# A decoder on one core: order of norm, turns and features at the beginning, and the first queries by band at the entry of the first cross-attention

## The reference, cut to what matters

```
x = x + L0_attn(layernorm(x))                 # linear attention, 16 heads of 8, cumulative sums over time
x = x + L0_xattn(layernorm(x), ctx, mask)     # softmax cross-attention, 16 heads, 256 keys per batch
x = x + L0_ffn(layernorm(x))                  # 8 experts, top 2, two loops
x = x + L1_attn(layernorm(x))                 # state-space scan
x = x + L1_xattn(layernorm(x), ctx, fside, mask)
x = x + L1_ffn(layernorm(x))                  # quantised feed-forward

# L0_attn: q, k, v, g = heads(x Wq), heads(x Wk), heads(x Wv), sigmoid(x Wg + bg)
# qf = softplus(q) * (g + 1e-6); kf = softplus(k)
# num = qf . cumsum(kf v^T); den = qf . cumsum(kf) + 1e-6; out = (num / den) Wo
# L0_xattn: softmax(q k^T / sqrt(8), key mask) v Wo
```

## Time and profile before

| | us |
|---|---|
| three runs | 608.24, 608.61, 612.67 |
| median of the runs | 608.61 |
| the profiled execution | 611.73 |
| its span, first to last instruction | 610.0 |

### The profile page before, as it was taken

The page is one execution under the profiler, slowest core; times in us unless marked ns, Lnnn a source line. Parts: engine busy times, 40 slices in busy tenths (PEclk is TensorE's granted clock), DMA queues, the critical chain, the costliest instruction groups (busy, mean ns, idle before and its releaser), DMA issues.

```text
span 610.0 us, 9155 instructions
## 1 busy us (share of the span) xinstructions
PE 526.7 (86%) x3260; PEld 298.6 (49%) x3268; DVE 452.4 (74%) x1175; ACT 263.2 (43%) x455; POOL 134.5 (22%) x101
## 2 busy tenths in 40 slices
PE   3997799999999999999999944655668999999886
PEld 1344666665666566566665500222224655555433
DVE  6599667676575366676456789999996778889786
ACT  5531256556433144243243346555521454444553
POOL 8443000000000000040000018899990100000100
PEclk9999799999998899999999985987788999999899
DMA  5000070000010000100000000000001000000001
GB/s 131 24 16 1 18 225 3 1 2 2 6 38 1 1 0 2 34 6 1 1 0 2 1 0 0 0 0 1 1 0 44 2 1 2 2 2 1 2 5 30
DMA packets 10768, 9.26 MB, mean 15 GB/s; under 512 B 2050, under 2 KB 9540, under 8 KB 10724
## 3 DMA queue, kind: packets, MB, share of 16 engines
q1 hardware_dynamic: 10724, 8.69, 5.0%
HBM read 6.98 MB, written 0.52 MB: 12 GB/s over the span
## 4 chain that ended last, share of the span: by engine, by line
PE 66%; DVE 23%; issue 5%; ACT 4%; POOL 2%; POOLq 0%; DVEq 0%; ACTq 0%
PE PS L1154 18%; PE PS L716 10%; PE PS L1180 9%; PE PS L779 5%; DVE PS L1713 5%; DVE VA L1726 5%; PE PS L764 3%; PE PS L755 3%; DVE PS L1719 2%; PE PS L692 2%; PE PS L736 2%; PE PS L455 1%; PE PS L287 1%; PE PS L433 1%; PE PS L789 1%
## 5 line engine op out<-in xcount | busy, mean ns | idle before, releaser
L1154 PE MATMUL PS<-XNT,KSA 128*128 128x512 f32 x256 | 121.5, 609 | 0.0
L941 ACT ACTIVATE E<-PS 128x512 f32<-128x512 f32 x128 | 71.2, 596 | 67.2 <-PE PS L764 41.7
L1168 DVE TENSOR_TENSOR E<-E,PS 128x512 f32<-128x512 f32 x64 | 43.9, 687 | 58.5 <-ACT E L1162 57.5
L1162 ACT ACTIVATE E<-PS 128x512 f32<-128x512 f32 x64 | 38.1, 597 | 108.4 <-PE PS L1154 108.2
L764 PE MATMUL PS<-QM,KP 32*128 32x256 f32 x512 | 81.3, 399 | 0.8 <-ACT E L941 0.8
L716 PE MATMUL PS<-KP,QP 32*128 32x256 f32 x512 | 78.6, 412 | 0.4 <-ACT QP L908 0.4
L1180 PEld LDWEIGHTS PS<-KSA,E 128*128 128x128 f32 x512 | 62.4, 192 | 16.8 <-issue 15.5
L1154 PEld LDWEIGHTS PS<-XNT,KSA 128*128 128x128 f32 x256 | 46.2, 195 | 42.8 <-issue 42.8
L1180 PE MATMUL PS<-KSA,E 128*128 128x128 f32 x512 | 62.4, 275 | 0.4 <-DVE XN L1389 0.4
L716 PEld LDWEIGHTS PS<-KP,QP 32*128 32x128 f32 x512 | 51.5, 191 | 20.8 <-issue 10.3
L292 PE MATMUL PS<-KSA,select 128*128 128x512 bf16 x62 | 24.9, 489 | 41.3 <-ACT KSA L1614 31.2
(11 more groups left out here) (280 smaller groups left out, 859.6 us busy)
## 6 DMA issues: line engine op xcount, KB each, us to landing
KSA<-in_w SPq DMA_DIRECT2D x2, 1024.0 KB, 6.9
X<-in_x SPq DMA_DIRECT2D x2, 256.0 KB, 3.3
SCR<-in_ctxT SPq DMA_DIRECT2D x1, 512.0 KB, 5.6
KP<-OT SPq DMA_DIRECT2D x16, 32.0 KB
SCR<-in_fside SPq DMA_DIRECT2D x1, 512.0 KB, 4.6
KP<-QM SPq DMA_DIRECT2D x16, 32.0 KB
out_x<-X SPq DMA_DIRECT2D x8, 64.0 KB, 1.5
wx<-in_w_x SPq DMA_DIRECT2D x1, 384.0 KB, 6.6
```

What stands on the lines that cost most here:

```text
L941: act.activation(slot(m, j), weight_bank(m, j), ACT.Exp).then_inc(sig("exps"), 1)
L1154: ins = pe.matmul(bank(2 * (g % 3) + o), w[:, e, c * P:(c + 1) * P], XNT[:, tokens_of(p)], start=True, stop=True)
L1162: act.activation(E6[:, 4 + g % 2, :], bank(2 * (g % 3)), ACT.Silu).then_inc(sig("silu"), 1)
L1168: dve.tensor_tensor(E6[:, g % 4, :], E6[:, 4 + g % 2, :], bank(2 * (g % 3) + 1), ALU.mult)\
```

## The change

At the beginning, VectorE does half 0's statistics and variance, half 1's statistics alone, half 0's tiles, and only then half 1's aggregation, variance and tiles. ScalarE computes half 0's root ahead of any key clearing, `by_head` ahead of half 1's root, and clears bands 0 and 1 behind the first copy, band 2 behind the second, and band 3 behind `pair(0)`. TensorE issues 16 products of the identity with itself (128x128, float32) ahead of the first turn; the second half's turn moves behind `features(0)`, and `context_keys` behind `features(1)`.

At the entry for L = 0, TensorE issues ten 128x512 bf16 products of the identity ahead of the turns and three behind them (`turn_ident`, into bank 7), behind two waits (`x_self`, `const_late`). `queries(0)` is replaced by `first_queries` of bands 0 and 1, as for L = 1, and of bands 2 and 3 after the scores. `turn_mixed(pe, 1)` moves behind the scores, which wait for `weighed_sum` instead (VectorE has read banks 3 to 5). ScalarE takes the queries in four copies, with `take_mixed(act, 1)` between the second and the third.

```diff
         def entry_variance(dve, ch, e, half):
             s = slice(4 * half, 4 * half + 4)
-            if e == 0:
-                dve.wait_ge(sig(("x_first", "x_second")[half]), 16)
             for j in range(s.start, s.stop):
                 ins = dve.bn_stats(st[:, j, :], X[:, j, :])
             ch.link(ins)
+            entry_spread(dve, ch, half)
+        def input_stats(dve, half):
+            dve.wait_ge(sig(("x_first", "x_second")[half]), 16)
+            for j in range(4 * half, 4 * half + 4):
+                ins = dve.bn_stats(st[:, j, :], X[:, j, :])
+            ins.then_inc(sig("input_stats"), 1)
+        def entry_spread(dve, ch, half):
+            s = slice(4 * half, 4 * half + 4)
             for j in range(s.start, s.stop):
                 ins = dve.bn_aggr(mv[:, j, :], st[:, j, :])
...
+        def turn_ident(pe, n):
+            for _ in range(n):
+                pe.matmul(bank(7), identb[:, :], identb[:, :].unsqueeze(1).to_broadcast([P, 4, P]),
+                          start=True, stop=True)
...
             features(0)
+            entry_turn(pe, 0, 1)
+            features(1)
             context_keys(pe)
-            features(1)
...
                 pair(b)
                 if b == 0:
+                    keys_clear(act, (3,))
                     keys_take(act, 0)
...
             def first_queries(gs):
-                pe.wait_ge(sig("xnt"), 2 * 5 + 1)
+                pe.wait_ge(sig("xnt"), 2 * (1, 5)[L] + 1)
                 for g in gs:
                     if g >= 2:
-                        pe.wait_ge(sig("query_taken"), g - 1)
-                    pe.matmul(first_query(g), WP[:, 1, g, :], XNT[:, 0:S], start=True, stop=True)\
+                        pe.wait_ge(sig("query_taken"), L * (NG - 1) + g - 1)
+                    pe.matmul(first_query(g), WP[:, L, g, :], XNT[:, 0:S], start=True, stop=True)\
                         .then_inc(sig("query_part"), 1)
...
-                if i == 0 and L == 1 and b == 0 and g < NG - 1:
-                    pe.wait_ge(sig("query_taken"), g + 1)
+                if i == 0 and b == 0 and g < NG - 1:
+                    pe.wait_ge(sig("query_taken"), L * (NG - 1) + g + 1)
...
             if L == 1:
                 turn_over(pe, 2, 16)
+            else:
+                pe.wait_ge(sig("x_self"), 1)
+                pe.wait_ge(sig("const_late"), 1)
+                turn_ident(pe, 10)
             entry_turn(pe, L + 1, 0)
-            if L == 0:
-                queries(0)
+            if L == 1:
+                turn_over(pe, 2, 2)
             else:
-                turn_over(pe, 2, 2)
-                first_queries((0, 1))
+                turn_ident(pe, 3)
+            first_queries((0, 1))
...
             else:
-                turn_mixed(pe, 1)
+                pe.wait_ge(sig("weighed_sum"), NT)
             for i in range(HG):
                 scores(0, i)
             if L == 0:
+                turn_mixed(pe, 1)
+            first_queries((2, 3))
+            if L == 0:
                 project_mixed(pe, 1)
                 context_values(pe)
-            else:
-                first_queries((2, 3))
             queries(1)
...
             entry_take(act, L + 1, 0)
+            for g in range(NG):
+                act.wait_ge(sig("query_part"), L * NG + g + 1)
+                ins = act.activation(QP[:, g, 0:S], first_query(g), ACT.Identity, bias=rowbias[:, L, 0, g:g + 1],
+                                     scale=DH ** -0.5)
+                if g < NG - 1:
+                    ins.then_inc(sig("query_taken"), 1)
+                if g == 1 and L == 0:
+                    take_mixed(act, 1)
+                if g == 1 and L == 1:
+                    entry_root(act, ch, 2, 1)
+            ins.then_inc(sig("queries"), 1)
             if L == 0:
-                take_queries(0)
-                take_mixed(act, 1)
                 context_scalar(act)
                 entry_root(act, ch, 1, 1)
...
             pe.wait_ge(sig("ident"), 1)
+            for _ in range(16):
+                pe.matmul(bank(0)[:, 0:P], ident[:, :], ident[:, :], start=True, stop=True)
             entry_turn(pe, 0, 0)
-            entry_turn(pe, 0, 1)
             self_tensor(pe)
...
             exp_and_ln(act)
+            entry_root(act, ch, 0, 0)
+            by_head(act)
+            entry_root(act, ch, 0, 1)
+            entry_take(act, 0, 0)
             keys_clear(act, (0, 1))
-            entry_root(act, ch, 0, 0)
-            entry_root(act, ch, 0, 1)
-            by_head(act)
-            entry_take(act, 0, 0)
             entry_take(act, 0, 1)
-            keys_clear(act, (2, 3))
+            keys_clear(act, (2,))
...
-            entry_variance(dve, ch, 0, 0)
-            entry_variance(dve, ch, 0, 1)
+            input_stats(dve, 0)
+            dve.wait_ge(sig("input_stats"), 1)
+            entry_spread(dve, ch, 0)
+            input_stats(dve, 1)
             entry_norm(dve, ch, 0, 0)
+            dve.wait_ge(sig("input_stats"), 2)
+            entry_spread(dve, ch, 1)
             entry_norm(dve, ch, 0, 1)
```

More of the change, by code:

```diff
@@ L903, in take_queries @@
             def take_queries(b):
-                act.wait_ge(sig("queries_psum"), L * (B - 1) + b + 1)
+                act.wait_ge(sig("queries_psum"), L * (B - 1) + b)
                 t = slice(b * S, (b + 1) * S)
```

## The result

The changed kernel takes 605.27 us in the median of 20 runs (599.4 to 608.19), the kernel before 607.8 in as many runs beside them (605.33 to 612.67). The ratio is 0.9943, with a 95% interval of 0.9921 to 0.9965: about 3.5 us, 0.6%, less than the one per cent that the prediction took for what can be told from no change; the two medians themselves differ by 2.5 us. The median of the changed kernel lies inside the predicted range, 1.8 us above the forecast. The profiled execution took 607.26 us with a span of 604.5; the one of before had 611.73 and 610.0, so the two profiles differ by 5.5 us in the span, more than the medians do.

What follows compares the result with a forecast made beforehand. The prediction took TensorE to bound the kernel from the cross-attention rounds on. Gains of 2.2 us at the beginning and 2.9 at the entry sum to 5.1, so 608.6 - 5.1 = 603.5 us, range 601.5 to 607.0.

Steps and rivals of the forecast that it cites:

- The beginning's first steps: 0 to 28 us: first tiles 8.7, first copy 9.8, features(0) 10.4, sums done 29.9; gain 2.2 us.
- The warm-up: Beginning: 32 instructions of identity products on TensorE from 1.55 us, ending by 9.2, nearly hidden by the root.
- the clock's rise: Beginning: TensorE reaches 2.4 GHz by 8.4 us, so features(0) takes 2.9 us, not 5.2 to 5.4.
- The slower rival: Beginning: too slow warm-up products hold TensorE's queue and delay the first turn; kernel takes 612.2 us; chance 0.04.
- The pause: 18.6 to 22.1 us: TensorE idles 3.5 us before the first outer sum and its clock falls, costing up to 3.4 us.
- the first rival: Pause at 18.6 to 22.1 us: no fall or a milder one; beginning gives 3.2 us, whole 6.1, 602.4; chance 0.20.
- The entry: 62.8 to 76 us, first cross-attention entry: fillers and queries by bands bring queries(1) 2.9 us earlier.
- the sum of 5.1: Whole kernel: 2.2 us from the beginning plus 2.9 us from the entry, taken off the median time.
- The fall at the entry: First entry, behind a 2.0 us pause: lower clock loses 1.0 to 2.5 of the 2.9 us; 605.2 us; chance 0.20.
- so if TensorE enters the rounds earlier by some time, the whole later kernel moves by it: Cross-attention rounds from 76 us: TensorE-bound with unchanged order, so the whole 5.1 us lead reaches the end.
- gone by 150: Sign of error: a gain at 76 us that is gone by 150 would mean the rounds are not TensorE's.
- the scale: Whole kernel: expected profiled 606.6 us was carried to the median by subtracting 3.1 us, giving 603.5.

Runs made afterwards that it cites:

- the second look: The kernel before, unchanged, run and profiled a second time: 607.25 us, profiled span 605.5.
- entry-only: The kernel before with the entry's edits alone, the beginning left as before: 605.87 us, ratio 0.9978 to the kernel before.
- beginning-only: The kernel before with the beginning's edits alone, the entry left as before: 607.64 us, ratio 0.9984 to the kernel before.

## Why the prediction was right

**The beginning's first steps** came out as worked: first tiles end 8.49 us (8.7 said), first copy 9.36 (9.8), features(0) 10.08 and 2.98 long (10.4 and 2.9), first pair 15.74 (16.3), second pair 20.75 (21.65), GpSimd's first sum ready 21.66 (22.1), sums done at 29.26 (29.9). Gain 2.87 us there against 2.2.

**The warm-up** ended at 7.0 us, not "by 9.2": 32 instructions in 5.44 us, 0.170 each, inside the bounds of 0.123 to 0.265. The mis-sized term is the clock's rise, taken as late as 8.4 us; it came at 4.95, and at 4.85 to 7.40 in the other traces with this warm-up. Nothing on the path waited for it: the turns start at 8.55 with VectorE's last tile as their releaser. The slower rival began at 0.24 us an instruction and was far off.

**The pause** was there, 3.40 us (3.5 said), and the clock fell behind it, at 22.0 us for 3.4, and in the second profile at 22.8. The kernel with one bias product, the same program up to there, shows the same 3.40 us without a fall; of six traces with this pause it is the only one. So the forecast holds for most executions and the first rival for some; in its trace filling the pause gave 1.1 us at 35 us.

**The entry** gave 2.98 us from the beginning's shift at the turns (59.83 against 62.81), then 8.03 us from turns to queries(1) where 11.20 stood: 3.17 us, 2.9 said. The small copy came 0.73 us after the queries (0.62), maxima followed the division at once. At queries(1) 6.15 us against 5.1 of the sum. But 11.20 us is the longer of two: against the second look, 10.34, the entry gives 2.3 us. Over the four pairs of a profile of before and one of the changed kernel the rounds start 4.5 to 6.2 us earlier, on average 5.4, so the sum of 5.1 was right in size. The fall at the entry happened in one profile of two (1.23 us, within "1.0 to 2.5"), and in three of the nine traces of all kernels with the ten fillers. Here belongs the Trainium skill, "TensorE: Matmul & The Clock Gate", section "Why this matters for your kernels", which counsels against pauses only longer than this one. The first profile agrees (pause 1.94 us, clock 1.00 at the entry); the second does not (1.93 us, half rate at 60.60), nor does the second entry (1.94 us before 461.25 us, then 2.08 us for four instructions of queries instead of 1.13). The measurement decides: behind a pause of this length the clock fell in some executions and not in others. At the second entry, 16 fillers and 1.94 us of pause, it fell in 12 of 13 traces.

**What the sum missed** is the way from the rounds to the clock on the wall. The step that failed is "so if TensorE enters the rounds earlier by some time, the whole later kernel moves by it". It holds for one pair of profiles: the gain at 76 us is not gone by 150, and the mark "gone by 150" did not occur. Over executions it does not hold in full: of 4.5 to 6.2 us at the rounds the spans of the four pairs keep 5.5, 6.7, 1.0 and 2.2, and the ratio gives 3.5. The rest went to falls of the clock far from the edit, at the context halves (1.7 us each; both are in all four profiles of the changed, entry-only and beginning-only kernels, and in one of the two of before), near 449 us and at the second entry. The other step is the scale: the profile of before was a long execution of its kind (611.73 against a median of 607.8), three falls of 1.6 us each heavier than the second look ahead of 210 us. The text took its distance to the median as a constant of 3.1 us and carried the sum across, which the medians, 605.27 and 607.8, bear out only by half. That the number still came within 1.8 us is in part luck: the base of 608.61, from three runs, was 0.8 us above the median of 20, which hides as much of the 2.6 us by which the gain was overestimated.

Whether the changed kernel has the falls at the context halves more often than the one before is open, and so is why it should: two profiles of each do not tell. The runs' mean clock goes with their time: of the changed kernel's 20, four had 0.959 and spans of 597.5 to 597.7, most 0.940 to 0.949 and 601.0 to 605.7. No profile caught one of the short ones, so which falls they lack was not seen.

## What to carry to other kernels

Work a gain out where it arises and check it in the trace there, but price what reaches the end by how often the clock falls in work that has nothing to do with the edit: two profiles of the same kernel differed by 4.5 us, more than this change gives. Where a reordering rests on full rate, test it without the warm-up as well; here it is then worse than the old order. And look at one-row bias products and short pauses behind which the clock falls before moving anything else: the kernel with one wide bias product had a median 7.3 us under the changed one's and by the ratios was some 5.4 us faster, more than this change gave. Of that 2.0 us are shown to be the shorter products; that the edit prevents the two falls, 3.8 us between the profiles, is likely but not shown.

## What the runs showed of the chip that was not expected

- TensorE's clock fell without any idle time before it: behind four pairs of a full and a one-row product, 20.00 of 20.00 us busy, it reads 0.50 for 3.4 us, and four 512-wide instructions take 3.31 us instead of 1.72.
- The same pause is answered in either way: 3.40 us with a fall (3.50 us for four instructions; five traces) and without (1.98 us; one); 1.93 to 1.94 us likewise (2.08 or 1.91 us for the queries against 1.13; a fall in three of nine traces at the first entry, in 12 of 13 at the second).
- Work ahead of the first useful product raises the clock 17 us earlier (4.95 against 22.4 us; over all traces 4.85 to 7.40 with the warm-up, 21.0 to 22.9 in the old order and 30.1 in the new order without it), but in at least one execution the clock fell again at 10.6 us and stayed for 20.5 us, which cost 7 us.
- The printed clock column reads 1.00 before the first change of the clock (at 9.4 to 21.7 us in the earlier trace rows), while durations of 1.71 us for a projection say 1.2 GHz.
